# A two-layer decoder forward pass: context rotation placed in the query stage, key-weight products interleaved in row tiles

## The chip, the cores and the metric

One of the eight cores of a Trainium2 chip runs the whole program in one launch. The metric is device time in microseconds (us), the median over several executions.

## The reference, cut to what matters

Two decoder layers work on x of 8 batches x 112 rows x 512 columns, with a context of 8 x 375 x 128. Each layer is grouped attention, attention to the context, and a feed-forward part. The change touches the end of the first attention (its output projection) and the query side of the first attention to the context. Written per head h (16 of them):

```python
q   = layernorm(x) @ Wq[h].T                # 512 -> 128
q_r = (q @ w_kc_q[h]) @ W_qr[h]             # 128 -> 384 -> 64
k_r = rotate(ctx) @ W_kr[h]                 # 128 -> 64, ctx rotated by position
p   = softmax(q_r @ k_r.T)
o   = (p @ rotate(ctx)) @ ...               # then w_kc_kv and Wo
```

The kernel folds the weights: C[h] = w_kc_q[h] @ W_qr[h], M[h] = Wq[h].T @ C[h], q_r = xn @ M[h], and qx[h] = q_r @ W_kr[h].T, which multiplies the rotated context directly. The context, rotated by cosine and sine tables, is needed in two layouts: by columns (`kvT`, 128 x 8 x 375) for the scores, and by rows (`kvr`, 125 x 3 x 8 x 128) for the values.

## The kernel before

Five engine programs are written out by hand as lists of stages and meet through semaphores: `done(...)` counts one up behind an instruction, `upon(...)` waits for that count. Within an engine the order of the code is the order of execution, so a wait holds up everything behind it. There is no scheduler.

Activations and weights that go through `mm3` are split into a high part (rounded by ScalarE, L289 or L669) and a rest (subtracted by VectorE, L675, or for weights by GpSimd, L294), and a product is three matmuls (L248, L249, L250): high by high, high by rest, rest by high. Weights stream from memory by the SP queue (`load`, L282) into three staging buffers `stg`, and the split pieces go into three slots `HL`.

The stages around the change, in order:

1. **First attention** (`pe_att0`). When its last value product is done, SP issues the tables `tabT`, `tabK` and the context `kvT`, `kvr` (L2227 to L2230), and then the next weight loads.
2. **First output projection** (`pe_o0` by `pe_out`, `act_o0`, `dve_o0`, `pool_o0`). There are 16 chunks of 128 rows of the weight, c = 0 to 15, and 7 tiles of 128 rows of x. For c = 0 to 11 TensorE runs over all 7 tiles (21 matmuls a chunk); then, tile by tile, it does chunks 12 to 15 (12 matmuls a tile) and four transposes of the tile before it. Chunk c needs `o_lo(c)` of VectorE (L675), which needs `o_hi(c)` of ScalarE (L669); there are four slots, so `o_hi(c)` waits for TensorE's chunk c - 4. VectorE and ScalarE are done with chunks 0 to 3 before the stage's own functions begin with chunk 4. Behind each finished tile VectorE adds the residual (L712) and normalizes (L305 to L315; `xn` is L315), TensorE transposes, ScalarE rounds (L327) and VectorE takes the rest (L331).
   The rotation of the context runs here: in `dve_o0` one batch of `kvT` (L744, L745, L747, L749) stands between `o_lo(c + 4)` and `o_lo(c + 5)` for c = 2 to 9, and in `pool_o0` one batch of `kvr` (L766, L767, L769, L771) stands between the weight splits. Both engines first wait for the tables and the context to land.
3. **Query stage** (`pe_q`, `act_q`, `dve_q`, `pool_q`). Ten steps over eight pairs of heads, software pipelined: step `st` makes C of pair `st` (L793), M of pair `st - 1` (L810), and for pair `st - 2` the query (24 matmuls, L841, in two halves of 448 columns, the C and M matmuls woven in between) and its products with the key weights `Krh` (the *key-weight products*: 2 halves x 2 heads x 3 matmuls by `mm3`). The two heads of a pair lie in rows 0 to 63 and 64 to 127 of `Krh` and `qrh`, so each product uses 64 rows of TensorE. Between a half's query and its key-weight products stand ScalarE's rounding (L889) and VectorE's rest (L917). The results go to banks 5, 6, 7 and again 5, and are copied out by VectorE (L929, the even head) and ScalarE (L901, the odd one).
4. **Context attention** (`pe_x`), which reads `kvT` and `kvr`.

The statement that picks the bank and, with it, the wait of the fourth product:

```python
bank = 5 + (2 * half + e_) % 3
if half == 1 and e_ == 1:
    e.wait_ge(*upon("dve_q", "o", hp, 0))
```

Of the kernel before, what the change touches and what calls it, by code (L numbers as in the profile page):

```python
# [8 lines left out]
R = mybir.dt.float32r  # L9
# [64 lines left out]
def build(nc, g):  # L74
# [8 lines left out]
    with ExitStack() as ctx:  # L83
# [74 lines left out]
        Krh = [at(f"Krh{i}", [128, 2, 128], R, o) for i, o in enumerate((rSCR + 16384, rSCR + 17408, rSCR))]  # L158
        qrh = [at(f"qrh{i}", [128, 2, HT], R, rSCR + (18432, 2048)[i]) for i in range(2)]
# [574 lines left out]
        def dve_o0(e):  # L734
            for c in range(12):
                o_lo(e, "o0", c + 4)
                if 2 <= c < 10:
                    b = c - 2
                    i = b % 2
                    tm = ctm[i]  # L740
                    if b == 0:
                        e.wait_ge(*upon("sp_ct", 1))
                        e.wait_ge(*upon("sp_ck", 1))
                    e.tensor_tensor(tm[0:64, :], kvT[64:128, b, :], tabT[64:128, 1, :], A.mult)  # L744
                    e.tensor_tensor(tm[64:128, :], kvT[0:64, b, :], tabT[0:64, 1, :], A.mult).then_inc(*done("dve_ctx", "r", b))  # L745
                    e.wait_ge(*upon("dve_ctx", "r", b))
                    e.tensor_tensor(kvT[:, b, :], kvT[:, b, :], tabT[:, 0, :], A.mult).then_inc(*done("dve_ctx", "c", b))  # L747
                    e.wait_ge(*upon("dve_ctx", "c", b))
                    e.tensor_tensor(kvT[:, b, :], kvT[:, b, :], tm[:, :], A.add).then_inc(*done("dve_ctx", "k", b))  # L749
            for t in range(NT):  # L750
                residual(e, "o0", t)
                ln_front(e, "lnx", t, xn[t % 2][:, :], ("pe_ln", "lnx", t - 2) if t > 1 else None)
                if t:
                    ln_lo(e, "lnx", t - 1, t - 1)
            ln_lo(e, "lnx", NT - 1, NT - 1)

        def pool_o0(e):
            e.wait_ge(*upon("sp_ct", 1))
            e.wait_ge(*upon("sp_ck", 1))
            for c in range(12):  # L760
                if c % 2 and 15 + c // 2 < 20:
                    rest_w(e, 15 + c // 2)
                if 2 <= c < 10:
                    b = c - 2
                    tk = ckm[b % 2]
                    e.tensor_tensor(tk[:, :, 0:64], kvr[:, :, b, 64:128], tabK[:, 1, :, 0:64], A.mult)  # L766
                    e.tensor_tensor(tk[:, :, 64:128], kvr[:, :, b, 0:64], tabK[:, 1, :, 64:128], A.mult).then_inc(*done("pool_ctx", "r", b))  # L767
                    e.wait_ge(*upon("pool_ctx", "r", b))
                    e.tensor_tensor(kvr[:, :, b, :], kvr[:, :, b, :], tabK[:, 0, :, :], A.mult).then_inc(*done("pool_ctx", "c", b))  # L769
                    e.wait_ge(*upon("pool_ctx", "c", b))  # L770
                    e.tensor_tensor(kvr[:, :, b, :], kvr[:, :, b, :], tk[:, :, :], A.add).then_inc(*done("pool_ctx", "k", b))  # L771
# [9 lines left out]

        def pe_q(e):
            def C_of(hp):
                for e_ in range(2):
                    k = piece["kq", 2 * hp + e_][0]
                    w = stg[k % NSTG]
                    e.wait_ge(*upon(f"sp_stg{k % NSTG}", k))
                    if hp:
                        e.wait_ge(*upon("act_q", "C", hp - 1, e_))
                    else:  # L790
                        e.wait_ge(*upon("dve_ln", "lnx", NT - 1, "lo"))
                    for c in range(3):
                        last = e.matmul(PS[:, e_, 0:64], w[:, c * 128:c * 128 + 128], w[:, 384 + c * 64:448 + c * 64],  # L793
                                        start=c == 0, stop=c == 2)
                        if c == 2:
                            last.then_inc(*done("pe_q", "C", hp, e_))
                        yield
                    freed[k] = "pe_q", "C", hp, e_

            def M_of(hp):  # L800
# [3 lines left out]
                e.wait_ge(*upon("act_q", "C", hp, 1))  # L804
# [18 lines left out]
            for st in range(10):  # L823
# [25 lines left out]
                for _ in side:  # L849
                    pass  # L850
                for half in range(2):
# [3 lines left out]
                    for e_ in range(2):  # L855
                        bank = 5 + (2 * half + e_) % 3
                        if half == 1 and e_ == 1:
                            e.wait_ge(*upon("dve_q", "o", hp, 0))
                        elif hp:
                            e.wait_ge(*(upon("act_q", "o", hp - 1, half) if e_ else upon("dve_q", "o", hp - 1, half)))  # L860
                            if half == 0 and e_ == 0:
                                e.wait_ge(*upon("act_q", "o", hp - 1, 1))
                        r0 = slice(64 * e_, 64 * e_ + 64)
                        kr, qr = Krh[hp % 3], qrh[half]
                        mm3(e, PS[:, bank, 0:HT], kr[r0, 0, :], kr[r0, 1, :], qr[r0, 0, :], qr[r0, 1, :], True,
                            True).then_inc(*done("pe_q", "k", hp, half, e_))

        def act_q(e):
            e.wait_ge(*upon("dve_ctx", "k", 7))
            e.wait_ge(*upon("pool_ctx", "k", 7))  # L870
            for st in range(10):
                if st < 8:
                    for e_ in range(2):
                        if st > 1 and e_ == 0:
                            e.wait_ge(*upon("pe_q", "M", st - 2))
                        e.wait_ge(*upon("pe_q", "C", st, e_))
                        e.activation(Cf[st % 2][:, e_ * 64:e_ * 64 + 64], PS[:, e_, 0:64], ACT.Copy).then_inc(*done("act_q", "C", st, e_))
                        if e_ == 0:
                            if st > 2:
                                e.wait_ge(*upon("pe_q", "k", st - 3, 1, 1))  # L880
                            k = piece["kq", 2 * st][0]
                            e.activation(Krh[st % 3][:, 0, :], stg[k % NSTG][:, 576:704], ACT.Copy).then_inc(*done("act_q", "K", st))
# [13 lines left out]
                if st > 1:  # L896
                    hp = st - 2
                    for half in range(2):
                        h = 2 * hp + 1
                        e.wait_ge(*upon("pe_q", "k", hp, half, 1))  # L900
                        e.activation(qx_at(half, h), psv(5 + (2 * half + 1) % 3), ACT.Copy).then_inc(*done("act_q", "o", hp, half))  # L901
            for k in piece["ox", 0][:1] + piece["ox", 1][:1] + piece["ox", 2][:1]:
                round_w(e, k)

        def dve_q(e):
            e.wait_ge(*upon("pool_ctx", "k", 7))
            for st in range(10):
# [16 lines left out]
                if st > 1:  # L924
                    hp = st - 2
                    for half in range(2):
                        h = 2 * hp
                        e.wait_ge(*upon("pe_q", "k", hp, half, 0))
                        e.tensor_copy(qx_at(half, h), psv(5 + (2 * half) % 3)).then_inc(*done("dve_q", "o", hp, half))  # L929

        def pool_q(e):
            for i in range(3):
# [1513 lines left out]
```

## Time and profile before

| | us |
|---|---|
| median of 3 executions | 1849.4 |
| lowest, highest | 1849.09, 1850.43 |
| the profiled execution, its own time | 1854.74 |
| span of the profiled execution | 1853.0 |

| engine | busy us | share of the span | instructions |
|---|---|---|---|
| PE (TensorE matmul) | 1670.4 | 90% | 9652 |
| PEld (weight load) | 1375.3 | 74% | 9652 |
| DVE (VectorE) | 1089.7 | 59% | 1829 |
| ACT (ScalarE) | 705.4 | 38% | 1207 |
| POOL (GpSimd) | 663.6 | 36% | 370 |

The span is that of the profiled execution alone, which ran a few microseconds longer than the median. Busy shares are means over all stages. PE's 90% does not say that TensorE bounds each stage; the page's row of 40 slices shows a stretch in the 8th and 9th slice where PE falls to 7 and 8 tenths while POOL stands at 9.

### The profile page before, as it was taken

Reading aid. Unit: us, or ns where it says so; the run is one execution under the profiler, and the core shown is the slowest. Engines: PE = TensorE matmul, PEld = TensorE weight load, DVE = VectorE, ACT = ScalarE, POOL = GpSimd, SP = SyncE. Lnnn points to the kernel's source line nnn. Section 1 sums busy time; section 2 is a strip of 40 time slices with the busy share of each in tenths; the row PEclk is TensorE's granted clock in tenths of the full one; section 3 lists DMA queues with packets and bytes.
Section 4 is the critical chain, followed back from the end, with each engine's and each line's share of the span. In section 5 each row is a group of like instructions: output and inputs, shape, how many; then the busy total and the mean of one; then the engine's idle time right before and its main releaser. Section 6 shows DMA issues by size and latency. Waiting matters only on the chain.

```text
span 1853.0 us, 24251 instructions
## 1 busy us (share of the span) xinstructions
PE 1670.4 (90%) x9652; PEld 1375.3 (74%) x9652; DVE 1089.7 (59%) x1829; ACT 705.4 (38%) x1207; POOL 663.6 (36%) x370
## 2 busy tenths in 40 slices
PE   5998999779999999974787999899878899999999
PEld 4897667568778887753576998687657788877887
DVE  5544564962277665687575765636476655555455
ACT  2112554212376664424351114623253433434342
POOL 2962442900000003599763763322241232222221
PEclk9998999979999999996898999999899999999999
DMA  4210003113231103500000110011000111111111
GB/s 127 69 58 1 2 2 107 42 41 111 67 103 45 46 12 123 188 12 0 1 0 1 58 52 29 11 46 33 19 19 29 40 46 52 57 46 40 57 55 43
DMA packets 28019, 87.48 MB, mean 47 GB/s; under 512 B 4090, under 2 KB 4090, under 8 KB 27655
## 3 DMA queue, kind: packets, MB, share of 16 engines
q1 hardware_dynamic: 27908, 85.94, 14.4%
q8 instruction: 77, 1.26, 0.3%
q14 instruction: 34, 0.28, 0.0%
HBM read 84.10 MB, written 1.84 MB: 46 GB/s over the span
## 4 chain that ended last, share of the span: by engine, by line
PE 73%; DVE 12%; ACT 6%; POOL 4%; issue 3%; DMA 2%; SPq 0%; ACTq 0%; DVEq 0%; POOLq 0%
PE PS L248 16%; PE PS L250 15%; PE PS L249 15%; PE PS L253 5%; PE PS L948 4%; PE PS L966 4%; PE PS L841 3%; PE PS L515 2%; PE PS L1284 1%; PE PS L1519 1%; DMA kvr<-in_ctxK 1%; ACT Sk L583 1%; DVE XT L675 1%; PE PS L1507 1%; ACT PT L575 1%
## 5 line engine op out<-in xcount | busy, mean ns | idle before, releaser
L294 POOL TENSOR_TENSOR HL<-stg,HL 128x1024 fp32r<-128x1024 f32 (+2 forms) x109 | 237.0, 2176 | 864.1 <-ACT HL L289 837.1
L248 PE MATMUL PS<-XT,HL 128*128 128x448 f32 x608 | 225.8, 371 | 10.7 <-DVE XT L331 8.4
L250 PE MATMUL PS<-XT,HL 128*128 128x448 f32 x608 | 224.1, 369 | 0.0
L249 PE MATMUL PS<-XT,HL 128*128 128x448 f32 x608 | 224.1, 369 | 0.0
L289 ACT ACTIVATE HL<-stg 128x1024 fp32r<-128x1024 f32 (+2 forms) x109 | 102.7, 945 | 308.2 <-PE PS L250 288.0
L248 PE MATMUL PS<-HL,XT 128*128 128x512 f32 (+1 forms) x380 | 141.1, 371 | 23.1 <-DVE XT L675 21.7
L249 PE MATMUL PS<-HL,XT 128*128 128x512 f32 (+1 forms) x380 | 137.9, 363 | 0.0
L250 PE MATMUL PS<-HL,XT 128*128 128x512 f32 (+1 forms) x380 | 137.7, 362 | 0.0
L248 PEld LDWEIGHTS PS<-XT,HL 128*128 128x128 f32 x608 | 115.4, 190 | 23.0 <-DVE XT L331 7.8
L249 PEld LDWEIGHTS PS<-XT,HL 128*128 128x128 f32 x608 | 115.5, 190 | 9.9
L250 PEld LDWEIGHTS PS<-XT,HL 128*128 128x128 f32 x608 | 115.3, 190 | 9.7
L2088 DVE SCALAR_TENSOR_TENSOR Hh<-PS,sml,Hh 128x448 fp32r<-128x448 f32 x64 | 43.2, 683 | 107.0 <-ACT Hh L1982 106.9
L248 PEld LDWEIGHTS PS<-HL,XT 128*128 128x128 f32 (+1 forms) x380 | 72.1, 190 | 39.2 <-DVE XT L675 15.0
L248 PE MATMUL PS<-HL,Ph 128*128 128x512 f32 x224 | 91.2, 407 | 3.7 <-DVE ACC L2111 1.8
L948 PE MATMUL PS<-kvT,QO 128*112 128x375 f32 x256 | 93.1, 487 | 1.5 <-ACT Sx L985 0.8
L999 DVE TENSOR_REDUCE nm<-PS 112x2 f32<-112x750 f32 x64 | 60.1, 940 | 55.9 <-PE PS L948 55.9
L648 POOL TENSOR_TENSOR Sk<-Sk,rc 112x896 f32<-112x896 f32 x32 | 53.3, 1684 | 102.6 <-DVE rc L630 102.6
L675 DVE TENSOR_TENSOR XT<-QO,XT 128x896 fp32r<-128x896 f32 x32 | 49.0, 1557 | 68.5 <-ACT XT L669 68.5
L249 PE MATMUL PS<-HL,Ph 128*128 128x512 f32 x224 | 88.2, 394 | 0.0
L250 PE MATMUL PS<-HL,Ph 128*128 128x512 f32 x224 | 88.1, 393 | 0.0
L966 PE MATMUL PS<-PX,kvr 125*128 125x224 f32 x384 | 83.9, 355 | 0.0
L1548 POOL TENSOR_TENSOR Sb<-Sb,rc 112x896 f32<-112x896 f32 x32 | 53.6, 1684 | 74.9 <-DVE rc L1543 74.9
(296 smaller groups left out, 3943.7 us busy)
## 6 DMA issues: line engine op xcount, KB each, us to landing
stg<-in_wst SPq DMA_DIRECT2D x85, 512.0 KB, 3.5
stg<-in_wst SPq DMA_DIRECT2D x16, 352.0 KB, 3.1
stg<-in_wst SPq DMA_DIRECT2D x16, 320.0 KB, 3.1
wsum<-in_wfc SPq DMA_DIRECT2D x8, 512.0 KB, 4.6
wsum<-in_wpj SPq DMA_DIRECT2D x8, 512.0 KB, 3.6
raw<-in_wfc SPq DMA_DIRECT2D x8, 512.0 KB, 3.9
stg<-in_wst SPq DMA_DIRECT2D x16, 256.0 KB, 2.5
raw<-in_wpj SPq DMA_DIRECT2D x7, 512.0 KB, 4.8
```

The lines of the kernel that those rows point to most:

```text
L248: e.matmul(out, lh, rh, start=start, stop=False)
L249: e.matmul(out, lh, rl, start=False, stop=False)
L250: return e.matmul(out, ll, rh, start=False, stop=stop)
L253: return e.transpose(out, in_, C("ident", n)[:, 0:n])
L289: e.activation(slot(k)[:, 0, 0:n], stg[k % NSTG][:, 0:n], ACT.Copy).then_inc(*done("act_w", k))
L294: e.tensor_tensor(slot(k)[:, 1, 0:n], stg[k % NSTG][:, 0:n], slot(k)[:, 0, 0:n].bitcast(F), A.subtract).then_inc(*done("pool_w", k))
L675: e.tensor_tensor(XT[:, 1, c % 4, :].rearrange("p (b s) -> p b s", b=NB), o_src(c, n), hi.bitcast(F), A.subtract).then_inc(*done(f"dve_{ta ...
L841: last = e.matmul(out, Mhl[i][:, a, kc, :], XT[:, c, kc, hs], start=kc == 0 and j == 0, stop=kc == 3 and j == 2)
L948: last = e.matmul(PS[0:S, bank + e_, 0:L], QO[:, 1 + st // 4, 2 * (st % 4) + e_, :], kvT[:, b, :], start=True, stop=True)
L966: last = e.matmul(PS[:, 6 + u % 2, 0:2 * S], kvr[:, c, u // 4 % 8, :], PX[u % 2][:, :, c, :], start=c == 0, stop=c == 2)
L999: e.tensor_reduce(nm[:, st % 4, :], PS[0:S, bank:bank + 2, 0:L], AX.X, A.max, negate=True).then_inc(*done("dve_x", "nm", st))
L1548: e.tensor_tensor(Sb[k][:, :, :], Sb[k][:, :, :], b8(rc[:, k, :]), A.mult).then_inc(*done(f"pool_{tag}", "p", u))
```

## The change

The context's rotation leaves the first output projection. `pool_o0` is only the five weight splits, `dve_o0` only the chunks. VectorE rotates one batch of `kvT` at the end of each query step 1 to 8 (`rotate_columns`); GpSimd rotates all eight batches of `kvr` at the start of `pool_q` (`rotate_rows`), which has no wait other than for the landed data. `pe_x` gets the waits for both.

In the query stage the key-weight products of a half's two heads alternate matmul by matmul (L864 now), each head into a bank of its own out of four (5, 6, 7, 1). For that, both C products of a pair share bank 0 and one ScalarE copy of 128 columns takes the place of two of 64, and C of a step waits for the copy of both heads of the step before. ScalarE rounds the key weights first in a step, not between the two copies. `Krh2` and `qrh1` move from the table's space to that of the weight slot `HL1`, since the tables now live on.

```diff
         def dve_o0(e):
             for c in range(12):
                 o_lo(e, "o0", c + 4)
-                if 2 <= c < 10:
...
-                    e.tensor_tensor(kvT[:, b, :], kvT[:, b, :], tm[:, :], A.add).then_inc(*done("dve_ctx", "k", b))
...
         def pool_o0(e):
-            e.wait_ge(*upon("sp_ct", 1))
-            e.wait_ge(*upon("sp_ck", 1))
-            for c in range(12):
...
+            for k in range(15, 20):
+                rest_w(e, k)
...
+        def kbank(half, e_):
+            return (5, 6, 7, 1)[2 * half + e_]
...
-                        e.wait_ge(*upon("act_q", "C", hp - 1, e_))
+                        e.wait_ge(*upon("act_q", "C", hp - 1))
...
-                        last = e.matmul(PS[:, e_, 0:64], w[:, c * 128:c * 128 + 128], w[:, 384 + c * 64:448 + c * 64],
+                        last = e.matmul(PS[:, 0, e_ * 64:e_ * 64 + 64], w[:, c * 128:c * 128 + 128], w[:, 384 + c * 64:448 + c * 64],
...
-                    for e_ in range(2):
-                        bank = 5 + (2 * half + e_) % 3
-                        if half == 1 and e_ == 1:
-                            e.wait_ge(*upon("dve_q", "o", hp, 0))
-                        elif hp:
...
-                        mm3(e, PS[:, bank, 0:HT], kr[r0, 0, :], kr[r0, 1, :], qr[r0, 0, :], qr[r0, 1, :], True,
-                            True).then_inc(*done("pe_q", "k", hp, half, e_))
+                    if hp:
+                        e.wait_ge(*upon("dve_q", "o", hp - 1, half))
+                        e.wait_ge(*upon("act_q", "o", hp - 1, half))
+                    kr, qr = Krh[hp % 3], qrh[half]
+                    for j, (a, c) in enumerate(((0, 0), (0, 1), (1, 0))):
+                        for e_ in range(2):
+                            r0 = slice(64 * e_, 64 * e_ + 64)
+                            last = e.matmul(PS[:, kbank(half, e_), 0:HT], kr[r0, a, :], qr[r0, c, :], start=j == 0, stop=j == 2)
+                            if j == 2:
+                                last.then_inc(*done("pe_q", "k", hp, half, e_))
...
         def dve_q(e):
-            e.wait_ge(*upon("pool_ctx", "k", 7))
...
+                if 1 <= st <= 8:
+                    rotate_columns(e, st - 1)
 
         def pool_q(e):
+            e.wait_ge(*upon("sp_ct", 1))
+            e.wait_ge(*upon("sp_ck", 1))
+            for b in range(NB):
+                rotate_rows(e, b)
             for i in range(3):
                 rest_w(e, piece["ox", i][0])
...
         def pe_x(e):
             e.wait_ge(*upon("dve_q", "o", 7, 1))
             e.wait_ge(*upon("act_q", "o", 7, 1))
+            e.wait_ge(*upon("dve_ctx", "k", 7))
+            e.wait_ge(*upon("pool_ctx", "k", 7))
```

GpSimd at the first output projection, before (a row is line, operation, output, inputs, shape; `ckm` is the rotation's scratch tile, `HL` the weight slots):

```order
L294 TENSOR_TENSOR HL_57<-stg_54,HL_57 128x1024
L766 TENSOR_TENSOR ckm_100<-kvr,tabK 125x3x64
L767 TENSOR_TENSOR ckm_100<-kvr,tabK 125x3x64
L769 TENSOR_TENSOR kvr<-kvr,tabK 125x3x128
L771 TENSOR_TENSOR kvr<-kvr,ckm_100 125x3x128
L294 TENSOR_TENSOR HL_58<-stg_55,HL_58 128x1024
```

and the same place of the changed kernel:

```order
L294 TENSOR_TENSOR HL_57<-stg_54,HL_57 128x1024
L294 TENSOR_TENSOR HL_58<-stg_55,HL_58 128x1024
L294 TENSOR_TENSOR HL_59<-stg_56,HL_59 128x1024
L294 TENSOR_TENSOR HL_57<-stg_54,HL_57 128x1024
L294 TENSOR_TENSOR HL_58<-stg_55,HL_58 128x1024
L764 TENSOR_TENSOR ckm_100<-kvr,tabK 125x3x64
```

The five splits stand together, and the rows' rotation follows the last of them without a weight split in between.

VectorE at the end of query step 2 and the start of step 3 in the changed kernel (`qrh`, `Mhl`: rests of the query and of M; `QO<-PS`: the copies of the key-weight products; L755 to L760: the rotation):

```order
L915 TENSOR_TENSOR qrh_112<-PS,qrh_112 128x448
L920 TENSOR_TENSOR Mhl_107<-PS,Mhl_107 128x512
L927 COPY QO<-PS 128x4x112 x2
L755 TENSOR_TENSOR ctm_99<-kvT,tabT 64x375
L756 TENSOR_TENSOR ctm_99<-kvT,tabT 64x375
L758 TENSOR_TENSOR kvT<-kvT,tabT 128x375
L760 TENSOR_TENSOR kvT<-kvT,ctm_99 128x375
L909 TENSOR_TENSOR Krh_108<-stg_55,Krh_108 128x128
L915 TENSOR_TENSOR qrh_111<-PS,qrh_111 128x448
```

Four operations stand newly between the last copy of one step and the key weights' rest of the next.

## Rows read from the trace of the kernel before

**Rows 1.** Chain of waits, 296 to 525 us: start us, us, what.
```profile
300.35 21.66 DMA kvr<-in_ctxK
...
382.62 0.70 DVE x L712
...
407.12 3.41 DMA stg<-in_wst
```

**Rows 2.** Stretches: us, then PE, PEld, DVE, ACT, POOL busy (instructions), PEclk, DMA share, GB/s.
```profile
341.60:375.70 34.10, 19.58 (x70) 14.05 (x70) 33.53 (x27) 6.03 (x6) 31.20 (x23) 0.83 0.10 32
...
441.80:453.10 11.30, 10.65 (x65) 9.18 (x64) 3.20 (x6) 3.23 (x8) 0.00 (x0) 1.00 0.33 110
...
475.70:488.60 12.90, 12.25 (x65) 10.59 (x64) 3.20 (x6) 3.23 (x8) 0.00 (x0) 0.87 0.28 94
```

**Rows 3.** Timeline of PE, output projection: start, us, instruction [idle before, releaser].
```profile
303.58 0.39 PE L248 MATMUL PS<-HL,XT 128*128 128x512 f32 x1
...
341.43 0.39 PE L250 MATMUL PS<-HL,XT 128*128 128x512 f32 x1
```

**Rows 4.** Timeline of DVE, output projection.
```profile
314.35 1.09 DVE L675 TENSOR_TENSOR XT<-QO,XT 128x896 fp32r<-128x896 f32 x1 [3.67 <-ACT XT L669]
...
326.99 1.90 DVE L675 TENSOR_TENSOR XT<-QO,XT 128x896 fp32r<-128x896 f32 x1
...
374.02 0.55 DVE L749 TENSOR_TENSOR kvT<-kvT,ctm 128x375 f32<-128x375 f32 x1
```

**Rows 5.** Timeline of POOL, output projection: one batch of rows, and what follows.
```profile
337.23 0.92 POOL L766 TENSOR_TENSOR ckm<-kvr,tabK 125x192 f32<-125x192 f32 x1
...
341.53 3.24 POOL L294 TENSOR_TENSOR HL<-stg,HL 128x1024 fp32r<-128x1024 f32 x1
```

**Rows 6.** DVE and POOL: tile 0's residual and normalization, the latter beside GpSimd, a group.
```profile
378.65 0.69 DVE L712 TENSOR_TENSOR x<-PS,x 128x512 f32<-128x512 f32 x1 [2.08 <-PE PS L250]
...
380.94 0.55 DVE L315 TENSOR_SCALAR xn<-x,mv,rs 128x512 f32<-128x512 f32 x1
...
24.90 1.42 DVE L315 TENSOR_SCALAR xn<-x,mv,rs 128x512 f32<-128x512 f32 x1
...
23.65 2.38 POOL L294 TENSOR_TENSOR HL<-stg,HL 128x1024 fp32r<-128x1024 f32 x1 [3.70 <-ACT HL L289]
...
L331 DVE TENSOR_TENSOR XT<-PS,XT 128x512 fp32r<-128x512 f32 x35 | 23.9, 684 | 17.8 <-ACT XT L327 17.8
```

**Rows 7.** Timeline of DVE, start of the query stage and between two steps.
```profile
406.73 0.29 DVE L911 TENSOR_TENSOR Krh<-stg,Krh 128x128 fp32r<-128x128 f32 x1 [2.11 <-ACT Krh L882]
...
451.10 0.68 DVE L922 TENSOR_TENSOR Mhl<-PS,Mhl 128x512 fp32r<-128x512 f32 x1
...
455.81 0.29 DVE L911 TENSOR_TENSOR Krh<-stg,Krh 128x128 fp32r<-128x128 f32 x1 [2.96 <-ACT Krh L882]
```

**Rows 8.** Timeline of PE, end of a query step and start of the next.
```profile
449.98 0.47 PE L248 MATMUL PS<-qrh,Krh 64*128 64x448 f32 x2
...
451.24 0.47 PE L248 MATMUL PS<-qrh,Krh 64*128 64x448 f32 x1 [0.39 <-DVE qrh L917]
...
452.37 0.47 PE L248 MATMUL PS<-qrh,Krh 64*128 64x448 f32 x1 [0.26 <-DVE QO L929]
...
453.17 0.67 PE L841 MATMUL PS<-XT,Mhl 128*128 128x448 f32 x2
```

**Rows 9.** Timeline of PE, the last half of the query stage.
```profile
505.07 0.47 PE L248 MATMUL PS<-qrh,Krh 64*128 64x448 f32 x1 [0.54 <-DVE qrh L917]
...
505.58 0.36 PE L250 MATMUL PS<-qrh,Krh 64*128 64x448 f32 x1
505.60 0.46 PE L248 MATMUL PS<-qrh,Krh 64*128 64x448 f32 x1
```

**Rows 10.** Groups of PE instructions: name, shapes, xcount, busy us, mean ns, idle before.
```profile
L515 PE MATMUL PS<-Kt,QO 32*112 32x112 f32 x1024 | 34.2, 289 | 0.0
...
L1507 PE MATMUL PS<-Kt,QO 128*112 128x112 f32 x256 | 27.9, 263 | 1.7 <-DVE Sb L1575 1.2 <-ACT V L1462 0.6
```

More of the change, by code:

```diff
@@ new lines, in rotate_rows @@
+        def rotate_rows(e, b):
+            tk = ckm[b % 2]
+            e.tensor_tensor(tk[:, :, 0:64], kvr[:, :, b, 64:128], tabK[:, 1, :, 0:64], A.mult)
+            e.tensor_tensor(tk[:, :, 64:128], kvr[:, :, b, 0:64], tabK[:, 1, :, 64:128], A.mult).then_inc(*done("pool_ctx", "r", b))
+            e.wait_ge(*upon("pool_ctx", "r", b))
+            e.tensor_tensor(kvr[:, :, b, :], kvr[:, :, b, :], tabK[:, 0, :, :], A.mult).then_inc(*done("pool_ctx", "c", b))
+            e.wait_ge(*upon("pool_ctx", "c", b))
+            e.tensor_tensor(kvr[:, :, b, :], kvr[:, :, b, :], tk[:, :, :], A.add).then_inc(*done("pool_ctx", "k", b))
@@ L803, in M_of @@
                 e.wait_ge(*upon(f"sp_stg{k % NSTG}", k))
-                e.wait_ge(*upon("act_q", "C", hp, 1))
+                e.wait_ge(*upon("act_q", "C", hp))
                 if hp:
@@ L870, in act_q @@
-            e.wait_ge(*upon("pool_ctx", "k", 7))
             for st in range(10):
                 if st < 8:
[L873 to L882, printed above, removed]
+                    if st > 2:
+                        e.wait_ge(*upon("pe_q", "k", st - 3, 1, 1))
@@ new lines, in act_q @@
+                    k = piece["kq", 2 * st][0]
+                    e.wait_ge(*upon(f"sp_stg{k % NSTG}", k))
+                    e.activation(Krh[st % 3][:, 0, :], stg[k % NSTG][:, 576:704], ACT.Copy).then_inc(*done("act_q", "K", st))
+                    if st > 1:
+                        e.wait_ge(*upon("pe_q", "M", st - 2))
+                    e.wait_ge(*upon("pe_q", "C", st, 1))
+                    e.activation(Cf[st % 2][:, :], PS[:, 0, 0:128], ACT.Copy).then_inc(*done("act_q", "C", st))
@@ L900, in act_q @@
                         e.wait_ge(*upon("pe_q", "k", hp, half, 1))
-                        e.activation(qx_at(half, h), psv(5 + (2 * half + 1) % 3), ACT.Copy).then_inc(*done("act_q", "o", hp, half))
+                        e.activation(qx_at(half, h), psv(kbank(half, 1)), ACT.Copy).then_inc(*done("act_q", "o", hp, half))
             for k in piece["ox", 0][:1] + piece["ox", 1][:1] + piece["ox", 2][:1]:
+                if k == piece["ox", 2][0]:
+                    e.wait_ge(*upon("pe_q", "k", 7, 1, 1))
                 round_w(e, k)
         def dve_q(e):
-            e.wait_ge(*upon("pool_ctx", "k", 7))
             for st in range(10):
```

45 lines of the change are left out of this document (14 added, 31 removed).

## The prediction

> **What bounds the kernel now.** I read the stretches first, then the chain of waits, then the timelines of single engines. In the stretches, the second part of the first output projection stands out [rows 2]: of 34.1 us VectorE is busy 33.5 and GpSimd 31.2, while TensorE has 19.6 and its granted clock falls to a mean of 0.83. The chain of waits says how it came to this [rows 1]: the context's last transfer takes 21.66 us and lands at 322.0, and from there the chain runs through VectorE's rotation and chunk rests, one after another; the residual of tile 0 starts at 378.65 only [rows 6].
>
> VectorE's operations are long there because of GpSimd, not by themselves. The same chunk rest takes 1.09 us while GpSimd is idle and 1.90 us once GpSimd rotates; the last sum of the rotation, after GpSimd's end, takes 0.55 us [rows 4]. So both engines read from two tiles of on-chip memory and hold each other up, and TensorE waits behind them: its last unhindered matmul starts at 341.43 [rows 3].
>
> In the query stage TensorE is the bound, with two short waits in every step [rows 8]. After a step's query the first half's key-weight products start at 449.98; the second half's at 451.24, when its query is rounded (ScalarE, then VectorE); its odd head waits for a bank until 452.37; the next step starts at 453.17. A step is 11.30 us [rows 2].
>
> **The change, part by part.** The sum is made against the profiled execution's own 1854.74 us; the median of the runs is 1849.4, 5.3 lower, and the gain is taken off that.
>
> *1. TensorE in the output projection.* Nothing but the chunk rests stands on VectorE now. TensorE's chunk 1 starts at 303.58, and chunk 8's last matmul at 341.43 [rows 3]: eight chunks of 21 matmuls, 168 of them, in 37.85 plus one more spacing of 0.23, so 4.76 us a chunk. Unhindered, chunk 12 starts at 303.58 + 11 x 4.76 = 355.9. Its operands are ready by then, except those of chunk 15: its slot comes free at 355.9, and then 1.0 of rounding (ScalarE's six operations of 6.03 us [rows 2]) and 1.09 to 1.90 of the rest follow [rows 4], with two hand-overs of about 0.05. I take 1.90, since GpSimd rotates by then (below): 359.0. The first tile's matmuls of chunks 12 to 14 end at 355.9 + 9 x 0.23 = 358.0, so TensorE waits 1.0 and is done with the tile at 359.7. The residual of tile 0 starts at about 359.9, 18.7 earlier than now [rows 6]. The weights cover this: the five splits are no longer behind the 21.66 us transfer, and the last split (piece of chunks 14, 15) needs chunk 9's end at 346.4, 1 of rounding and 2.4 for the split [rows 6], so 350.
>
> *2. The normalization that follows.* Before, the residual of tile 1 starts at 382.62 [rows 1]. In the change it starts after tile 0's VectorE work, 2.84 from 378.65 to the normalization's end [rows 6], plus a hindrance h: 359.9 + 2.84 + h + 0.1. (Now it also waits for matmuls that the low clock made slow.) What hinders: GpSimd starts its rows at about 350.5, needs 4.30 us a batch [rows 5], 34.4 for eight and some more for its own waits, and so is busy until about 387, through nearly all of the normalization. Of VectorE's operations per tile only the normalization itself (L315) takes on-chip memory alone and is long; those with a PSUM operand are not hindered: the 35 rests L331 have a mean of 684 ns, their plain length, though some ran beside GpSimd [rows 6]. L315 takes 0.55 alone [rows 6]; at 24.90 it took 1.42, beside a GpSimd split that ended at 26.03 [rows 6], so it ended 0.29 after GpSimd. It loses what is left of GpSimd's current operation less 0.26. With two operations of 0.9 and two of 1.2 a batch that is (0.64^2 + 0.94^2)/(2.1 x 2) = 0.31 us on average, between 0 (GpSimd leaves gaps) and 0.94 (always the whole of the longest). Seven tiles, so h is 0.31 each, 2.2 in all, bounds 0 and 6.6. Residual 1 starts at 363.2: 19.4 earlier. Six further tiles lose 1.9. **Gain of both parts: 17.5 us**, bounds 13 and 20.
>
> The Trainium skill speaks against this placement: "SBUF — State Buffer", section Who interferes with whom, holds that the loser of the shared port is blocked for the whole of the other's instruction; taken at its worst each tile would lose 1.2, 8.4 in all, and the sum would be 6.2 less. By the row, part of L315's fixed time passes while it is blocked.
>
> *3. Start of the query stage.* The fourth weight piece is on the path: its load is issued at 407.12 and takes 3.41 [rows 1], behind VectorE's key-weight rest at 406.73, which had waited 2.11 for ScalarE [rows 7]. ScalarE now rounds the key weights before the first C product is done, so the load waits for that product alone. Estimated 0.8 us, bounds 0 and 2.1.
>
> *4. Key-weight products.* The half that counts is the second; the first is hidden by the rounding chain up to 451.24 [rows 8], before and after. Before: 451.24 to 453.17, 1.93 us. After: six matmuls in three pairs, no bank wait. What a pair costs is not in the trace for 64 rows. In the last half of the stage, where no bank was waited for, a head's three matmuls take 0.51 from the first start to the last, and the second head's first starts 0.02 after the first head's last [rows 9]: two row tiles do overlap at that seam. And where four row tiles alternate, a matmul of 112 columns costs 34.2/1024 = 33 ns, against 27.9/256 = 109 for the same width over 128 rows [rows 10]. So I take the pairs to cost what one head does: 0.51 + 0.02 to the last start, and 0.29 to the next step's start (as now from 452.37 + 0.51 = 452.88 to 453.17). 0.82 in place of 1.93 is 1.1 us. The next step also needs the rest of M, done at 451.78 [rows 7]: no new wait. Bounds: without any overlap six matmuls take 0.51 + 0.02 + 0.51 = 1.04 to the last start [rows 9], 1.33 in all, gain 0.6. Seven steps x 1.1 = 7.7; the last has no bank wait and gets 0.5 (1.04 down to 0.53). **8.2 us**, bounds 4.2 and 8.2.
>
> By the Trainium skill ("TensorE: Matmul & The Clock Gate", The mechanism, under row and column tiling) concurrent tiles start about 4 ns apart, not 20; with it the sum would be some 0.1 us better.
>
> *5. What is added at nothing.* VectorE's rotation, one batch a step: four operations of 0.55 [rows 4] with hand-overs, 2.4 us, GpSimd being done. It stands before the next step's key-weight rest, in an idle stretch of 2.96 [rows 7]. If that cover were gone, the next load and then the query's rest would be late; there is over 1 us more until the latter. The step gets shorter by 1.1, the idle time with it, and 2.4 is still covered with that second gap. Loads: three pieces in 10.2 us; a piece lands in about 3.4 and each slot has some 7. The copy of 128 columns in place of two of 64 is off the path, and the moved tiles are free by then. The waits of `pe_x` are met: the last batch of columns is rotated a step and a half before, the rows 100 us before.
>
> **Sum.** 17.5 + 0.8 + 8.2 = 26.5 us. Profiled: 1854.7 - 26.5 = 1828.2. Median: 1849.4 - 26.5 = 1822.9. From no change a measurement of this kernel can tell about 0.2%, 3.7 us.
>
> **The rivals.**
> - *Row tiles don't overlap for 64 rows.* The alternation then gives only the bank wait: 4.2 in place of 8.2, 1826.9. For it: the seam of 0.02 could be a record that starts while it still waits for the array. Against: the 33 ns group.
> - *The port costs more.* GpSimd and VectorE fall into step and each L315 loses up to 0.94: 4.4 us more, 1827.3. For it: during the rotation a chunk rest grew by 0.8 [rows 4]. Against: L315 is shorter, and at 24.90 it lost 0.87 against a much longer operation.
> - *The clock.* One query step ran 12.9 us at a mean clock of 0.87 in place of 11.3 at 1.00 [rows 2], after a run of like steps with TensorE 94% busy; the slow part is the 1.2 GHz level. If the denser steps lose or gain one such episode, 1.6 us either way; two more of them, 1826.1.
> - *Alternating row tiles is slower than before.* If TensorE had to finish a matmul before the other row tile may start, each would cost its whole 0.47 [rows 9], six of them 2.82 a half in place of 0.82. Both halves would pay: the second 2.0 x 8 = 16, the first 1.6 beyond its cover x 8 = 13. The sum is 26.5 - 29 = -2.5, 1851.9. It decides once a matmul costs over 0.44. Against it speaks all of rows 10.
> - *GpSimd isn't in the way at all*: 2.2 + 0.8 more, 1819.9.
>
> **How the numbers follow.** The forecast 0.60, no overlap 0.13, the port 0.12, the clock 0.08, GpSimd free 0.05, slower than before 0.02. The range takes in the first five, with the port and the missing overlap partly together (1849.4 - 18 = 1831), and half of the margin on the other side: 1818.5 to 1830.5. Faster by over 0.2%: all but the slower rival and its neighbourhood, 0.97; 0.015 for the same and 0.015 for slower.
>
> **What the profile after would show.** (1) TensorE without a wait from 303.58 to about 358, POOL busy without a break from 350 to 387. (2) L315 of about 0.9 on average in the seven tiles, the stage's last L331 ending near 387, 17.5 earlier than now. (3) Query steps of about 10.2 us, the second half's products 0.82 from first start to the next step. (4) VectorE's rotation operations at 0.55 each. (5) Context attention's first matmul near 480.7, 26.5 earlier than now, and nothing lost behind it. The prediction is wrong if steps stay at 10.7 or more, if the normalization's tiles take over 4 us each, or if a later stage gives time back.

## The result, and the profile after

| | before | after |
|---|---|---|
| median, us | 1849.39 (4 runs) | 1821.3 (4 runs) |
| lowest, highest | 1849.09, 1850.43 | 1816.57, 1821.75 |
| ratio, 95% interval | | 0.9841, 0.9824 to 0.9858 |
| profiled execution, own time | 1854.74 | 1821.46 |

28.1 us faster; 26.5 were forecast. The two profiled executions are 33.3 us apart. To see where, both traces are cut at the same events, each by its start in TensorE's timeline: the projection's first matmul, the first C product (which ends the projection here), and the first score matmul of context attention.

| us | before | after | gain |
|---|---|---|---|
| earlier stages, code unchanged | 298.68 | 296.13 | 2.5 |
| output projection with normalization | 106.09 | 87.09 | 19.0 |
| query stage | 102.42 | 91.77 | 10.7 |
| all later stages | 1345.8 | 1344.7 | 1.1 |

The first row is scatter: over the twelve further profiles below it lies between 292.2 and 298.4 with this code unchanged. So the two stages of the change gave about 29.7 in this pair of profiles, 2.3 of it by the granted clock (end of the section on the prediction), and nothing was given back behind them.

Stretches of the kernel after (us, then PE, PEld, DVE, ACT, POOL busy with instructions, PEclk, DMA share, GB/s); the first is the same 34.1 us as in [rows 2], the second one query step:

```profile
341.60:375.70 34.10, 32.90 (x150) 25.64 (x149) 20.59 (x39) 8.06 (x14) 28.41 (x32) 1.00 0.04 11
...
426.70:436.90 10.20, 9.82 (x64) 8.70 (x64) 5.29 (x11) 3.01 (x8) 0.00 (x0) 1.00 0.38 124
```

TensorE is busy 32.9 of 34.1 where it had 19.6, at full clock. The wait on the chunk rests, 14.5 us over the two stages before, is down to 0.2, and the one on VectorE's copy (1.8) is gone. TensorE's waits over both stages, after (in total, times, longest, us):

```profile
PE PS L253 <- DVE xn L315: 3.5, 2, 2.8
PE PS L864 <- DVE qrh L915: 3.2, 8, 0.5
PE PS L794 <- DVE XT L331: 1.5, 1, 1.5
PE PS L842 <- DVE Mhl L920: 1.4, 1, 1.4
PE PS L811 <- DMA stg<-in_wst: 0.9, 1, 0.9
...
PE PS L248 <- DVE XT L675: 0.2, 1, 0.2
```

Timeline of DVE after, around the first tiles, which answers to [rows 4, 6]:

```profile
354.64 1.09 DVE L675 TENSOR_TENSOR XT<-QO,XT 128x896 fp32r<-128x896 f32 x1 [2.98 <-ACT XT L669]
356.79 0.69 DVE L712 TENSOR_TENSOR x<-PS,x 128x512 f32<-128x512 f32 x1 [1.05 <-PE PS L250]
...
359.08 1.10 DVE L315 TENSOR_SCALAR xn<-x,mv,rs 128x512 f32<-128x512 f32 x1
360.10 0.68 DVE L712 TENSOR_TENSOR x<-PS,x 128x512 f32<-128x512 f32 x1
...
362.38 1.28 DVE L315 TENSOR_SCALAR xn<-x,mv,rs 128x512 f32<-128x512 f32 x1
...
366.53 0.61 DVE L315 TENSOR_SCALAR xn<-x,mv,rs 128x512 f32<-128x512 f32 x1
```

and POOL in the same stretch:

```profile
354.85 1.75 POOL L769 TENSOR_TENSOR kvr<-kvr,ckm 125x384 f32<-125x384 f32 x1
...
362.37 1.01 POOL L769 TENSOR_TENSOR kvr<-kvr,ckm 125x384 f32<-125x384 f32 x1
363.34 0.78 POOL L764 TENSOR_TENSOR ckm<-kvr,tabK 125x192 f32<-125x192 f32 x1
...
365.85 1.00 POOL L769 TENSOR_TENSOR kvr<-kvr,ckm 125x384 f32<-125x384 f32 x1
366.81 0.78 POOL L764 TENSOR_TENSOR ckm<-kvr,tabK 125x192 f32<-125x192 f32 x1
```

Chunk 15's rest starts 0.21 ahead of GpSimd's operation and takes its plain 1.09, and GpSimd's grows from 1.01 to 1.75. The normalization at 362.38 starts beside an operation that ends at 363.38 and ends 0.28 after it. From 366.53 on the two engines are in step: the normalization starts 0.3 before GpSimd's L769 ends, loses 0.06, and the next L764 takes 0.78 in place of 0.60.

Timeline of PE after, at a query step's end (answers to [rows 8]) and at the start of the stage (answers to [rows 1, 7]):

```profile
383.22 2.79 PE L794 MATMUL PS<-stg 128*128 128x64 f32 x12 [1.50 <-DVE XT L331]
386.47 2.81 PE L794 MATMUL PS<-stg 128*128 128x64 f32 x12 [0.46 <-ACT Cf L879]
390.20 2.18 PE L811 MATMUL PS<-Cf,stg 128*128 128x64 f32 x9 [0.91 <-DMA stg<-in_wst]
...
425.44 0.86 PE L864 MATMUL PS<-qrh,Krh 64*128 64x448 f32 x6
426.70 0.87 PE L864 MATMUL PS<-qrh,Krh 64*128 64x448 f32 x6 [0.39 <-DVE qrh L915]
427.50 0.69 PE L842 MATMUL PS<-XT,Mhl 128*128 128x448 f32 x2
```

The second half's products take 0.80 from first start to the next step, 1.93 before.

### The profile page after: what moved, and what is told of

It reads as the page before. It is cut to its first block, busy times and chain, and to the rows that moved or that the text cites. A ratio compares the mean times of both kernels' runs of the same rounds, so it can differ in the third digit from the quotient of the medians.

```text
span 1819.7 us, 24247 instructions
## 1 busy us (share of the span) xinstructions
PE 1651.7 (91%) x9652; PEld 1364.4 (75%) x9652; DVE 1065.9 (59%) x1829; ACT 703.5 (39%) x1199; POOL 653.8 (36%) x370
## 4 chain that ended last, share of the span: by engine, by line
PE 77%; DVE 9%; ACT 6%; POOL 5%; issue 3%; DMA 1%; SPq 0%; ACTq 0%; DVEq 0%; POOLq 0%
PE PS L248 17%; PE PS L249 16%; PE PS L250 16%; PE PS L253 5%; PE PS L954 4%; PE PS L972 4%; PE PS L842 3%; PE PS L515 2%; PE PS L1290 1%; PE PS L1525 1%; ACT Sk L583 1%; PE PS L1513 1%; ACT PT L575 1%; POOL Gb L1411 1%; PE PS L1305 1%
## 5 line engine op out<-in xcount | busy, mean ns | idle before, releaser
L248 PE MATMUL PS<-XT,HL 128*128 128x448 f32 x608 | 225.4, 371 | 10.7 <-DVE XT L331 8.4
L249 PE MATMUL PS<-XT,HL 128*128 128x448 f32 x608 | 223.7, 368 | 0.0
L248 PE MATMUL PS<-HL,XT 128*128 128x512 f32 (+1 forms) x380 | 138.6, 365 | 8.8 <-DVE XT L675 7.4
L249 PE MATMUL PS<-HL,XT 128*128 128x512 f32 (+1 forms) x380 | 135.9, 358 | 0.0
L250 PE MATMUL PS<-HL,XT 128*128 128x512 f32 (+1 forms) x380 | 135.8, 357 | 0.0
L248 PEld LDWEIGHTS PS<-XT,HL 128*128 128x128 f32 x608 | 115.2, 189 | 23.0 <-DVE XT L331 7.8
L249 PEld LDWEIGHTS PS<-XT,HL 128*128 128x128 f32 x608 | 115.2, 190 | 9.7
L675 DVE TENSOR_TENSOR XT<-QO,XT 128x896 fp32r<-128x896 f32 x32 | 45.0, 1432 | 99.4 <-ACT XT L669 99.4
L248 PE MATMUL PS<-HL,Ph 128*128 128x512 f32 x224 | 90.5, 404 | 3.7 <-DVE ACC L2117 1.8
L248 PEld LDWEIGHTS PS<-HL,XT 128*128 128x128 f32 (+1 forms) x380 | 70.9, 187 | 22.3 <-DVE XT L675 6.5
L249 PE MATMUL PS<-HL,Ph 128*128 128x512 f32 x224 | 87.5, 390 | 0.0
```

Of the source, the lines that this page charges most:

```text
L248: e.matmul(out, lh, rh, start=start, stop=False)
L249: e.matmul(out, lh, rl, start=False, stop=False)
L250: return e.matmul(out, ll, rh, start=False, stop=stop)
```

## The experiments

The runs of one chip share the runs of the kernel before: `e1_move`, `e2_tiles`, `e3_heads` and `e6_cols_o0` (before 1852.1 there); `c_after`, `e4_late`, `e7_early_m` and `e8_both` (1854.6); `e5_rows_o0`, `e9_cols_late` and `e10_best` (1852.8); `e11_splits_first` (1849.4). Each is given as its median (lowest to highest) and the ratio to the kernel before with its 95% interval. Medians of like kernels scatter by a few us, so verdicts on less rest on the stages of the profiles: "projection" and "query stage" as cut above. There is one profile of each kernel.

**The parts alone.** `e1_move` takes only the rotation's move, `e2_tiles` only the key-weight products:

```diff
# e1_move: the changed kernel with pe_q, act_q of before
-            return (5, 6, 7, 1)[2 * half + e_]
+            return 5 + (2 * half + e_) % 3
# e2_tiles: the kernel before with pe_q, act_q of the changed one
+            return (5, 6, 7, 1)[2 * half + e_]
```

> The rotation moved as in the change, the query stage's matmul order, banks and copies as before. Theory (the two parts add up, the output projection gives about 19 us in the profile, the rest is the query stage's): query steps stay at 11.3 us, the second half's products at 1.93 to the next step, tile normalizations as in the changed kernel; median about 1831. Rival (the parts need each other, as steps of 11.3 us would have hidden something): above 1836 or below 1826.

> Four banks, alternating heads and the new copies as in the change, the rotation left in the output projection. Theory: steps of 10.2 us, 0.8 to the next step, 8 to 10 us gained in the query stage, the stall of TensorE from 341 to 376 unchanged; median about 1840. Rival (overlap of row tiles appears only because VectorE or GpSimd are elsewhere): steps of 10.7 or more, 1844 or above.

`e1_move`: 1831.3 (1830.5 to 1833.4), ratio 0.9891 (0.9872 to 0.9910); projection 87.10, query stage 103.08. `e2_tiles`: 1839.5 (1837.4 to 1840.9), 0.9933 (0.9913 to 0.9953); projection 106.69, query stage 92.40. Each part gives its stage what it gives in both together, 19 and 10. (By the medians of that chip the parts give 20.8 and 12.6, and the changed kernel's like, `e3_heads` below, 29.8: the sum is off by the scatter.) TensorE in `e1_move`, at a step's end:

```profile
425.18 0.47 PE L248 MATMUL PS<-qrh,Krh 64*128 64x448 f32 x2
425.48 0.37 PE L249 MATMUL PS<-qrh,Krh 64*128 64x448 f32 x2
...
426.43 0.47 PE L248 MATMUL PS<-qrh,Krh 64*128 64x448 f32 x1 [0.38 <-DVE qrh L917]
...
427.56 0.47 PE L248 MATMUL PS<-qrh,Krh 64*128 64x448 f32 x1 [0.26 <-DVE QO L929]
```

Where no bank is waited for (425.18), the code has head 0's three matmuls ahead of head 1's, and yet both heads' L248 stand together ahead of both L249. That asks what the alternation does at all.

**Alternation or banks.** `e3_heads` keeps the four banks and turns the two loops round, so that head 0's three matmuls come first:

```diff
-                    for j, (a, c) in enumerate(((0, 0), (0, 1), (1, 0))):
-                        for e_ in range(2):
+                    for e_ in range(2):
+                        for j, (a, c) in enumerate(((0, 0), (0, 1), (1, 0))):
```

> The changed kernel, but a half's products head by head again, into the same four banks: the bank wait is gone, the alternation too. Theory (the alternation makes row tiles overlap): a half takes 1.04 from first to last start in place of about 0.5, steps are about 10.7, the last half 0.5 longer, median about 1825.3, 4 us above the changed kernel. Rival (all of the gain was the bank wait, six matmuls overlap anyway): steps of 10.2, no difference.

1822.3 (1820.1 to 1825.4), ratio 0.9842 (0.9820 to 0.9864), query stage 91.90: the changed kernel's own. Six matmuls in program order by heads take what the alternating ones do:

```profile
425.96 0.87 PE L864 MATMUL PS<-qrh,Krh 64*128 64x448 f32 x6
427.21 0.88 PE L864 MATMUL PS<-qrh,Krh 64*128 64x448 f32 x6 [0.39 <-DVE qrh L915]
```

The theory that alternation makes the overlap falls. What counts is a free bank for the fourth product, so that no wait stands between the heads. (The merged copy of C and the earlier rounding of the key weights were not tried apart from the banks; from the first C product to the first query matmul it is 11.92 without them, in `e1_move`, and 12.06 with them.)

**Where the port costs.** The port is here, as in the prediction, whatever VectorE and GpSimd hold each other up at when both read on-chip operands. `e6_cols_o0` leaves the columns' rotation in the projection beside the splits and the rows, `c_after` is the changed kernel once more, and `e4_late` holds the rows back until the normalization is done:

```diff
# e6_cols_o0, in dve_o0 (and none in dve_q)
+                if 2 <= c < 10:
+                    rotate_columns(e, c - 2)
# e4_late, in pool_q ahead of the rows
+            e.wait_ge(*upon("dve_ln", "lnx", NT - 1, "lo"))
```

> The changed kernel, but VectorE's rotation of the columns back between the chunk rests of the output projection, GpSimd's rows after the weight splits as in the change. Theory (the stall was the two engines blocking each other): VectorE alone needs 1.09 + 2.3 us a chunk, under TensorE's 4.76, so TensorE has no wait over 1 us before chunk 12 and the time is that of the changed kernel within 1.5 us, 1820 to 1823. Rival (VectorE's own load made the stall): chunk rests are late by 10 us or more in all, 1831 or above.

> The changed kernel again, as the yardstick for the three beside it: 1821 us, a spread of some 5 us down to 1816.6 as in its runs so far. Theory for the spread: steps of the query stage or other stretches with the granted clock at its lower level in some executions.

> The changed kernel with one wait more: GpSimd begins the rows' rotation only after the last normalized tile's rest. Theory (GpSimd's port costs the normalization 1.5 us, and nothing in the query stage): L315 takes 0.55 in all seven tiles, the stretch from tile 0's residual to the last rest is 1.5 us shorter, VectorE's columns take up to 1 us longer per batch in the first two or three steps but steps stay at 10.2; time 1.5 us below the changed kernel. Rival: the hindered columns delay a step, and the time is the same or higher.

`e6_cols_o0`: 1828.6 (1823.8 to 1831.8), ratio 0.9870 (0.9840 to 0.9899), projection 96.12: 9 us lost, where I had reckoned with 1.5. I had counted the operations at their plain length. DVE's timeline beside a GpSimd split (334.70 to 337.32) and at the end, beside the rows:

```profile
334.52 0.54 DVE L758 TENSOR_TENSOR ctm<-kvT,tabT 64x375 f32<-64x375 f32 x1
335.10 2.63 DVE L760 TENSOR_TENSOR kvT<-kvT,tabT 128x375 f32<-128x375 f32 x1
337.76 0.55 DVE L762 TENSOR_TENSOR kvT<-kvT,ctm 128x375 f32<-128x375 f32 x1
...
354.15 1.24 DVE L757 TENSOR_TENSOR ctm<-kvT,tabT 64x375 f32<-64x375 f32 x1
...
358.30 3.68 DVE L675 TENSOR_TENSOR XT<-QO,XT 128x896 fp32r<-128x896 f32 x2
```

TensorE waited 7.0 us in two waits for chunk rests.

`c_after`: 1818.7 (1815.8 to 1820.8), ratio 0.9816 (0.9794 to 0.9837), projection 87.08, query stage 91.75. `e4_late`: 1818.7 (1817.4 to 1824.5), ratio 0.9823 (0.9800 to 0.9846); L315 takes 0.55 in all seven tiles and the projection 85.82, so the port costs the changed kernel 1.3 there. The query stage is 0.7 longer (92.43). The rows do run beside the first columns' rotations now, and stretch operations of 0.55 to as much as 1.36, but the query's rest still finds VectorE idle:

```profile
398.19 0.62 DVE L915 TENSOR_TENSOR qrh<-PS,qrh 128x448 fp32r<-128x448 f32 x1 [1.67 <-ACT qrh L886]
```

TensorE's waits are those of `c_after`, and the steps from the first on last the same 10.17 to 10.21. What differs is the granted clock in the first step: TensorE runs at half of it (the 1.2 GHz level) until 17.2 us behind the first C product, in `c_after` until 15.7, and from the first query matmul to VectorE's rest of that step's second half it takes 11.00 in place of 10.15. `e6_cols_o0` has 16.9 and 10.89 with no rotation of columns in that stage at all. So the 0.7 is no price of the late rows' port. The net gain of 0.6 in the two stages is below what the medians tell.

`e9_cols_late` puts both edits together: VectorE has as much to do as in `e6_cols_o0`, but only the splits are beside it.

> VectorE's columns between the chunk rests as in the run with columns there, but GpSimd's rows wait until the normalization is over, so beside the columns GpSimd has only the weight splits. Theory (of the 7.0 us that TensorE waited in that run, the rows caused most): VectorE ends the last chunk rest about 5 us earlier, TensorE waits under 3 us, and the start of the query stage comes 5 to 7 us earlier in relation to the start of the projection. Rival (VectorE's own load): the wait stays at 7.

1822.6 (1820.2 to 1823.6), ratio 0.9837 (0.9812 to 0.9861); the projection takes 89.40 and TensorE waits 1.8 where it waited 7.0. Being blocked by the rows is 6.7 of the 9.0 us. The rest is not free: against `e4_late`, where the rows wait alike, the columns between the chunk rests still cost 3.6 (89.40 and 85.82), and four of their operations take 2.6 beside a split. No run has the columns there with GpSimd idle, so what VectorE's work alone would cost stays open.

**Rows in the projection, columns outside.** `e5_rows_o0` puts the rows back between the splits, as in the kernel before:

```diff
-            for k in range(15, 20):
-                rest_w(e, k)
+            for c in range(12):
+                if c % 2 and 15 + c // 2 < 20:
+                    rest_w(e, 15 + c // 2)
+                if 2 <= c < 10:
+                    rotate_rows(e, c - 2)
```

> The changed kernel, but GpSimd's rotation of the rows back between the weight splits of the output projection; VectorE's columns stay in the query stage. Theory (either engine's rotation alone leaves TensorE fed; only both at once block it): chunk rests of up to 1.9 us beside the rows, all covered by the 4.76 of a chunk, GpSimd done before or soon after the first tile's residual, L315 at 0.55 in nearly all tiles, TensorE's waits before the first tile under 2 us; the projection 1 us shorter than in the changed kernel. Rival (the rows alone hold up the chunk rests or the weight splits): waits of TensorE of 5 us or more.

1830.8 (1829.7 to 1831.9), ratio 0.9884 (0.9864 to 0.9903). My theory falls and its rival holds: the rows alone hold up the weight splits. L315 takes 0.55 in every tile and TensorE never waits for a chunk rest, but the last weight split comes at 361.03, where the changed kernel has it at 346.11. Two things make it late: the first split waits for the landed context, as in the kernel before (322.04; 308.03 after the change), and seven batches stand ahead of the last. POOL's timeline and TensorE's one long wait:

```profile
350.36 2.40 POOL L294 TENSOR_TENSOR HL<-stg,HL 128x1024 fp32r<-128x1024 f32 x1
...
361.03 2.34 POOL L294 TENSOR_TENSOR HL<-stg,HL 128x1024 fp32r<-128x1024 f32 x1
```

```profile
PE PS L248 <- POOL HL L294: 6.3, 1, 6.3
```

The projection takes 93.39; the weight loads behind it are late too, and the first query matmul comes 14.14 after the first C product (12.06 after the change). TensorE waits 2.9 us there for the load of M's piece.

**The start of the query stage.** The change brings nothing there: 12.06 us from the first C product to the first query matmul, 12.17 before. The C products of the second pair (386.47) are not wanted before the first M; the piece that M needs is loaded behind theirs. `e7_early_m` makes M of the first pair before C of the second, and orders the loads so; ScalarE and VectorE round M(0) first:

```diff
+        if hp == 1:
+            kinds += [("qx", 0), ("kq", 2), ("kq", 3)]
...
             def beside(st):
+                if st == 1:
+                    yield from M_of(0)
+                    yield from C_of(1)
+                    return
```

> The changed kernel with the first M product (and its weight piece, its rounding and its rest) ahead of the second pair's C products. Theory (at the start of the query stage the load of the first qx piece is on the path, since it waits for the second C product and takes 4.1): the wait of 0.9 for that load goes and the first query starts 2 to 4 us earlier; the C products of pair 1 fill the time of the rounding; 2 to 3 us below the changed kernel. Rival (the path is TensorE's low clock there, whatever the order): under 0.5 us.

1817.9 (1816.0 to 1820.5), ratio 0.9813 (0.9793 to 0.9834); 9.21 in place of 12.06, query stage 88.47, 3.3 less than after the change.

**Together.** `e8_both` is `e7_early_m` with `e4_late`'s wait, `e10_best` is `e7_early_m` with the rows of `e5_rows_o0`.

> Both of the former edits. Theory: they are on different stretches of the path and add: about 4 us below the changed kernel, 1817. Rival: GpSimd, now beside the start of the query stage, hinders VectorE's first rests of key weights and the gain of the early M shrinks: under 2.5 us.

> The rows in the output projection and the early first M product, both on top of the changed kernel. Theory: the projection 1 us shorter (no GpSimd beside the normalization), the query stage 3.2 shorter as in the run with the early M product, nothing given back to hindered columns: 4.5 us below the changed kernel, about 1816 where that is 1820.5. Rival: the rows hold up the splits and the gain of the projection is gone, 3 us at most.

`e8_both`: 1816.9 (1814.2 to 1820.6), ratio 0.9805 (0.9783 to 0.9828), both stages 175.36 against 178.83 for `c_after` on the same chip. That is 3.5 us, but `e7_early_m` alone has 175.57: on top of the early M the late rows bring 0.2, 0.8 in the projection less 0.6 in the query stage, where the full clock came back 13.6 us behind the first C product instead of 12.3. The medians (1816.9, 1817.9 and 1818.7) scatter by as much. `e10_best`: 1823.5 (1822.1 to 1826.2), 0.9846 (0.9825 to 0.9868): the early M gives its 3 us (query stage 88.88), the late split takes 6.30 again.

Whether the late split or the rows beside the chunk rests cost that, `e11_splits_first` tells: the same kernel with the first two splits ahead of the wait for the context, and then at most two batches between one split and the next, four in all ahead of the last.

```diff
+            rest_w(e, 15)
+            rest_w(e, 16)
+            rotate_rows(e, 0)
+            rest_w(e, 17)
+            rotate_rows(e, 1)
+            rotate_rows(e, 2)
+            rest_w(e, 18)
+            rotate_rows(e, 3)
+            rest_w(e, 19)
+            for b in range(4, NB):
+                rotate_rows(e, b)
```

> Edit: the early M (as in e7) with the rows' rotation back in the output projection, but so that no weight split stands behind a backlog of rows: splits 15, 16, rows 0, split 17, rows 1 and 2, split 18, rows 3, split 19, rows 4 to 7. Theory (late splits cost e10 its gain): the last split is done by about 350 (361 in the run with eight batches between), TensorE does not wait for GpSimd's split, the next weight loads are on time; GpSimd is done with the rows near 367, so that only the first two or three tiles of the normalization lose anything. Projection 85.5 to 86.5 us from its first matmul to the first C product (93.55 in e10, 87.1 in e7), query stage 88.5, together 174 to 175.5; own time 1814 to 1819, median some 2 us under e7's. Rival (what cost e10 was VectorE's chunk rests held up by the rows, 1.09 to 1.9 us each): the projection stays at 92 or more with waits for VectorE's rests, own time 1822 or more.

1819.7 (1815.4 to 1822.7), ratio 0.9830 (0.9811 to 0.9850). The last split is done at 351.05, GpSimd with the rows at 366.4, and L315 takes 0.70, 0.73 and then 0.55:

```profile
348.65 2.40 POOL L297 TENSOR_TENSOR HL<-stg,HL 128x1024 fp32r<-128x1024 f32 x1
...
365.37 1.01 POOL L783 TENSOR_TENSOR kvr<-kvr,ckm 125x384 f32<-125x384 f32 x1
```

TensorE's wait for a split is gone, although chunk rests take up to 2.90 beside GpSimd, and the projection takes 86.43 (93.55 in `e10_best`). So the late split was the cause, in `e5_rows_o0` too; how much of it was the wait for the context and how much the batches, the runs don't part. The query stage came to 89.37 where 88.5 was expected (the clock was back 14.1 us behind the first C product, 12.3 in `e7_early_m`), both stages to 175.80, and the median is not below that of `e7_early_m` or `e8_both`. All three orders of the rows behind an early M (175.57, 175.36, 175.80) are alike within what one profile can tell.

## Why the prediction was right

*1, TensorE in the projection: right.* From the first matmul to tile 0's residual it was 79.97 (298.68 to 378.65) and is 60.66 (296.13 to 356.79): 19.3, where 18.7 was forecast. Most of the difference is one choice of mine, worth 0.8: chunk 15's rest takes 1.09, not 1.90, since it started first and GpSimd's operation was the one to wait. The Trainium skill ("SBUF — State Buffer", Who interferes with whom) says of the pair that whoever issues first keeps the port, and these rows agree.

*2, the normalization: right in kind, its loss set too high.* The first tile's step to the second shrank from 3.97 (378.65 to 382.62) to 3.31, the clock being full, 0.66 gained as forecast. Behind that I forecast a loss of 1.9 in six tiles; it is 0.97 (22.15 before and 23.12 now, from tile 1's residual to the first C product), all told 1.5 us over the seven L315. The step that failed is the average over random meetings, (0.64^2 + 0.94^2)/(2.1 x 2). The engines do not meet at random: GpSimd's batch takes 3.30 alone (3.48 less the 0.18 by which L764 is held up; not the 4.30 of [rows 5], which VectorE's rotation had stretched), VectorE's tile 3.42 (`e4_late`), and after two tiles both run at 3.48. VectorE's slower round moves its normalization later in GpSimd's until it starts near the end of L769; from there it is GpSimd's next operation that is held up, and the two keep one pace. `c_after`, `e1_move` and `e3_heads` have the same seven durations within 0.02. The lock-in that I had named as the way to lose 0.94 a tile settles at the cheap end, 0.06. That rival's mechanism was there, its price was not. With it parts 1 and 2 gave 19.0 in place of 17.5. The same section of the Trainium skill, by which the loser is blocked for the whole of the other's instruction, is right on the block (362.38: until 0.28 after GpSimd's end); the 8.4 that I had drawn from it took every tile to meet a longest operation whole, and one of seven did (that at 362.38).

*3, the start of the query stage: wrong.* 0.8 was forecast, 0.1 measured (12.17, 12.06). The step that failed is taking the gain of one load for the gain of the path. The load that I called critical is indeed issued earlier (1.5 us behind the first C product's start, 2.4 before), but it is no longer the last: the chain after has the piece for the first M, which waits for the staging buffer of the first pair's second head:

```profile
383.22 2.81 PE PS L794 x12
386.04 4.11 DMA stg<-in_wst
390.20 3.69 PE PS L811 x16
```

I had asked what the fourth piece waited for and not what came behind it. `e7_early_m` shows what was to be had there, 2.9. The stage's first query step is 0.6 shorter all the same, for another reason: TensorE is back at full clock 15.8 us behind the first C product, 17.3 before. That was no part of the forecast; over the ten profiles without the early M it lies between 15.7 and 19.8.

*4, the key-weight products: size right, reason wrong.* 8.2 was forecast. Between the halves' second rounding points seven intervals shrank by 9.36 in all, 1.62 of which is the slow step of [rows 2]; the other 7.74 and the last half's 0.54 are 8.3. But by my account 4.2 was the bank wait and the rest the alternation. `e3_heads` shows that the alternation gives nothing: two row tiles overlap as soon as no wait stands between them. The row that told it stood in the prediction's own groups: 449.98 with x2 [rows 8] is both heads' first matmul, in code that runs them head by head. And the seam that I took for the array's, 505.58 and 505.60 [rows 9], was head 1 being released by VectorE's copy, which ends at 505.54:

```profile
504.93 0.61 DVE L929 COPY QO<-PS 128x448 f32<-128x448 f32 x1
```

So it is wrong that no bank was waited for in the last half. Both readings led to the same sum, which was luck; the time alone could not have told them apart.

*5, added at nothing: right.* VectorE's rotation in the query stage, after:

```profile
407.95 0.55 DVE L755 TENSOR_TENSOR ctm<-kvT,tabT 64x375 f32<-64x375 f32 x1
...
410.14 0.28 DVE L909 TENSOR_TENSOR Krh<-stg,Krh 128x128 fp32r<-128x128 f32 x1
411.85 0.62 DVE L915 TENSOR_TENSOR qrh<-PS,qrh 128x448 fp32r<-128x448 f32 x1 [1.42 <-ACT qrh L886]
```

1.42 of idle time is left behind it, and steps take 10.16 to 10.21 in all variants with this query stage.

*The clock* was a rival at 1.6 us either way, and it fell on the good side, with another 0.6 in the first step (3). Both profiles with steps of 11.3 have a slow one: the kernel before one of 12.92, `e1_move` one of 12.90 at another place and a shorter step of 11.52 for 9.90. None of the twelve profiles with steps of 10.2 has any. By the stages, 29.7 is 26.5, 1.5 more from parts 1 and 2, 0.7 less from part 3, 0.1 from part 4, and 2.3 from the clock. That the medians' 28.1 is 26.5 and 1.6 is chance, since the sum is finer than the measurement: on another chip the same two kernels were 35.9 apart (1854.62, 1818.73). That the slow step belongs to the kernels with the longer steps is read from fourteen profiles, two of them with such steps; nothing was tried that shows why.

## What to carry to other kernels

Two engines that read two on-chip operands each should be placed by who may wait: here the rotations of both engines cost 14.5 us of TensorE's time beside chunk rests on the critical path and, moved apart, 1.3 beside the normalization and nothing seen in a stage where VectorE idles. When work is moved out of a queue, look for the split or load queued behind it, and at what the queue waits for first: a split behind the wait for the context and seven batches cost 6.3 us, and an order with two splits ahead of that wait and at most two batches between the others cost none. Of matmuls in different row tiles, count the waits between them and not their order in the code.

## What the hardware showed that I had not expected

- Matmuls of 64 rows in different row tiles start out of the program's order: in `e1_move` head 1's L248 starts before head 0's L249, which stands ahead of it. The Trainium skill ("TensorE: Matmul & The Clock Gate", The mechanism, under row and column tiling) has matmuls start strictly in program order; these rows speak against that across row tiles, and agree with it within one.
- A blocked VectorE operation keeps only part of its own time behind the block: L315 (0.55 alone) ended 0.28 after GpSimd's operation. Whoever started first was not slowed (the chunk rest at 354.64: 1.09, as alone).
- Two engines with nearly equal periods (3.30 and 3.42) lock at 3.48, at which VectorE loses 0.06 a tile. At which end they would settle with other periods, no run shows.
- An operation of 64 x 375 that takes 0.55 took 2.64 beside a GpSimd split (323.15 in `e6_cols_o0`; such a split takes 2.4 alone).
